# 23 blocks of rows in place of 24 in a mixture of experts, with a loop of four rounds and a tail of seven blocks

## The chip, the cores and the metric

The kernel runs on one core of a Trainium2 chip. A core has five engines with instruction streams of their own: TensorE (PE) multiplies matrices into eight banks of PSUM, VectorE (DVE), ScalarE (ACT) and GpSimd (POOL) work element by element, and SyncE (SP) issues DMA transfers. They meet only at semaphores. The metric is the time on the device in microseconds (us) of one execution; the lower the better.

## The reference, cut to what matters

Two layers run over 1024 rows of 256 numbers: attention over a context, then a mixture of experts, and the same once more with other weights. The change is in the first mixture of experts:

```python
logits = x @ router_w.T                                  # 8 experts
probs = softmax(logits)
top_w, top_i = top_k(probs, 2)
top_w = top_w / sum(top_w)
for e in range(8):
    gate, up = bitlinear(x, gate_w[e]), bitlinear(x, up_w[e])     # 256 -> 512
    y_e = bitlinear(up * square(relu(gate)), down_w[e])           # 512 -> 256
    out = out + combine[:, e:e + 1] * y_e
# bitlinear: weights rounded to -1, 0, 1 over their mean magnitude; each row of x
# rounded to integers of -128..127 over its largest magnitude
```

Each row goes to two of eight experts, so 2048 pairs of row and expert are worked on.

## The kernel before

The pairs are sorted by expert and cut into blocks of 128; the last block of each expert is filled up. `NBLK` blocks are always worked through, whatever the routing gives, and the blocks behind the last one in use compute on spare rows. 2048 pairs fill 16 blocks exactly, and each of eight experts can leave one block partly filled.

A block j goes through these steps, each on its engine:

- POOL gathers its 128 rows from DRAM into `xg[j % 4]` (line 570). Its program is one straight list: in step j it scales the hidden rows of block j - 7 (line 565), gathers block j and stores y of block j - 8 (line 577), as far as these blocks exist.
- TensorE turns the rows (`turn_rows`, line 763), ACT copies them out (`rows`, line 1220), TensorE multiplies by gate and up (`gate_up`, line 781). The expert comes from a register, since routing is known only while the kernel runs.
- ACT takes the relu of the gate (`relus`, line 1225), DVE squares, multiplies by up and finds the largest magnitude of each row for the rounding (`hidden`, lines 1579 to 1587), POOL scales.
- TensorE turns the hidden rows (`turn_hidden`, line 789), ACT rounds them (`hidden_rows`, line 1229), TensorE multiplies by down (`down`, line 796), ACT scales y out of PSUM (`outputs`, line 1235), and POOL stores it to the row's place in `y_rows`. ACT writes the y of a block only when the store of the block two before has landed.

Gate and up of a block lie in PSUM banks 1 and 3 if the block is even, in 2 and 4 if it is odd; bank 0 takes turned rows, bank 5 turned hidden rows, bank 6 y.

TensorE runs a prologue for blocks 0 to 3, then a hardware loop (`pe.Fori`) over rounds of four blocks, then a tail. In the part for block j stand `turn_hidden(j)`, `turn_rows(j + 4)`, `gate_up(j + 3)` and `down(j)`. A round loads one word from `run_e` into a register (`run_of`, line 771), which holds the experts of seven blocks, three bits each, and `in_run` shifts them out. With 24 blocks the loop has five rounds (blocks 0 to 19) and the tail four blocks (20 to 23). The tail loads a word again and also the last block's expert from `block_ei` (line 767). DVE has a loop too, over blocks 4 to 23 in five rounds; ACT and POOL have straight lists.

Behind block 20 and block 21 TensorE's list holds the first two pieces of the next job: folding the weights of the second layer's attention (`fold_queries` line 812, `fold_values` line 826, `fold_keys` line 841, for eight units u). `fold_values(0)` writes bank 1 and `fold_keys(0)` banks 3 and 1, so the last block must not use these. `fold_keys(0)` waits until y of the last block has been copied; the other folds follow. ACT and DVE copy each fold out. SP loads the weights of folds 1, 2, 3, 4 and 6 when the rows of blocks 5, 8, 11, 14 and 17 have been turned, and when all of y has landed it loads y back by rows (`yg`, line 511), from which DVE forms the layer's result and its normalisation.

Of the kernel before, what the change touches and what calls it, by code (L numbers as in the profile page):

```python
# [9 lines left out]
P = 128  # L10
# [11 lines left out]
FF = 512  # L22
NBLK = 24
RUN = 7
XROW = 258
QMAX = 127.0
# [71 lines left out]
def build(nc, x, ctx_in, cst_in, sel_in, kv_in, router_w, ffn_w, fold_in,  # L98
          weight_t, scale, masks_t, router_dt, out):
    with ExitStack() as ctx:  # L100
# [3 lines left out]
        def sb(name, shape, dt=F32):  # L104
            n = int(np.prod(shape[1:])) * (2 if dt == BF16 else 4)
            at = place[0]
            place[0] = (at + n + 31) // 32 * 32
            places[name] = at
            return nc.alloc_sbuf_tensor_at(name, shape, dt, offset=at)
# [50 lines left out]
        block_ei = sb("block_ei", [P, NBLK], U32)  # L160
        run_part = sb("run_part", [P, NBLK // 4 - 1])
        run_e = sb("run_e", [P, NBLK // 4 - 1], U32)
        below2 = sb("below2", [P, NBLK, NE])
# [208 lines left out]
        def rows_back(b):  # L372
            return (gathered[b], 16 * (NBLK // 4) + 16) if b < 4 else (sorted_back[b - 4], 16)

# [88 lines left out]
        def _(sp):  # L463
# [42 lines left out]
            for par in range(2):  # L506
                sp.wait_ge(y_stored[par], 16 * (NBLK // 2))
            y_by_tile = y_rows[0:2 * NT * P].rearrange("(k t p) d -> p k t d", k=2, p=P)
# [101 lines left out]
        def _(pe):  # L610
# [165 lines left out]
            def gate_up(j, par, e):  # L776
                pe.wait_ge(xgT_ready, j + 2)
                pe.wait_ge(hid_done, j + 1)
                for k in range(2):
                    for m in range(2):  # L780
                        mm = pe.matmul(bank[1 + 2 * m + par][:], xgT[par][:, k * P:(k + 1) * P],  # L781
                                       W[:, bass.ds(e, 1), m, k * FF:(k + 1) * FF].rearrange("p a i -> p (a i)"), start=k == 0, stop=k == 1)
                mm.then_inc(gu_ready, 1)
# [65 lines left out]
            pe.wait_ge(runs_ready, 1)  # L849
            with pe.Fori(0, NBLK // 4 - 1) as i:  # L850
                word = run_of(i)
                for r in range(4):
                    j = 4 * i + r
                    e_up, e_down = in_run(word, r + 3), in_run(word, r)
                    turn_hidden(j, r)
                    turn_rows(j + 4, i + 1, r)
                    gate_up(j + 3, (r + 1) % 2, e_up)
                    down(j, r % 2, e_down)
            word, last = run_of(NBLK // 4 - 2), expert_of(NBLK - 1)
            for j in range(NBLK - 4, NBLK):  # L860
                e_down = in_run(word, j - NBLK + 8) if j < NBLK - 1 else last
                turn_hidden(j, j % 4)
                if j + 3 < NBLK:
                    gate_up(j + 3, (j + 1) % 2, last)
                down(j, j % 2, e_down)
                if j == NBLK - 4:
                    fold_queries(0)
                if j == NBLK - 3:
                    pe.wait_ge(hid_done, NBLK + 1)
                    fold_values(0)  # L870
# [263 lines left out]
        def _(act):  # L1134
# [87 lines left out]
            def relus(j, par):  # L1222
                act.wait_ge(gu_ready, j + 1)
                act.wait_ge(hid_done, j + 1)
                act.activation(relu[par][:], bank[1 + par][:], ACT.Relu).then_inc(relu_ready, 1)

# [11 lines left out]
            for j in range(4):  # L1238
                rows(j, j % 2, j)
                if j:  # L1240
                    relus(j - 1, (j - 1) % 2)
            for i in range(NBLK // 4 - 1):
                for r in range(4):
                    j = 4 * i + r
                    hidden_rows(j, r % 2)
                    rows(j + 4, r % 2, r)
                    relus(j + 3, (r + 1) % 2)
                    outputs(j, 2 * i + r // 2, r % 2, r)
            for j in range(NBLK - 4, NBLK):
                hidden_rows(j, j % 2)  # L1250
                if j + 3 < NBLK:
                    relus(j + 3, (j + 1) % 2)
                outputs(j, j // 2, j % 2, j % 4)
# [40 lines left out]
            for u in range(NU):  # L1294
                if u == NU - 2:
                    for par in range(2):
                        act.wait_ge(y_stored[par], 16 * (NBLK // 2))
                fold(u)
# [73 lines left out]
        def _(dve):  # L1372
# [189 lines left out]
            dve.sem_inc(block_w_ready, 1)  # L1562
            seventh = 4 * (NBLK // 4 - 2) + 1
            so_far = block_e[:, RUN - 1:RUN - 1 + seventh:4]
# [8 lines left out]
            def hidden(j, r):  # L1573
# [4 lines left out]
                dve.wait_ge(relu_ready, j + 1)  # L1578
                link(dve.scalar_tensor_tensor(hid[r][:], bank[1 + par][:], 0.0, relu[par][:], ALU.max, ALU.mult))  # L1579
                dve.tensor_tensor(hid[r][:], hid[r][:], bank[3 + par][:], ALU.mult).then_inc(hid_done, 1)  # L1580
                dve.wait_ge(hid_done, j + 3)
# [7 lines left out]
            for j in range(4):  # L1589
                hidden(j, j)  # L1590
            with dve.Fori(1, NBLK // 4) as i:
                link.enter(i - 1, 16)
                for r in range(4):
                    hidden(4 * i + r, r)
                link.leave(NBLK // 4 - 1, 16)

# [339 lines left out]
```

## Time and profile before

| | |
|---|---|
| median of 3 runs | 512.0 us (511.37 to 514.07) |
| profiled execution, on the device | 510.0 us |
| its span in the trace | 508.2 us |
| PE busy | 384.1 us, 76% of the span |
| DVE busy | 362.7 us, 71% |
| ACT busy | 216.9 us, 43% |
| POOL busy | 146.6 us, 29% |
| the blocks of the first experts | from the first gather at 135.4 us to the last store at 223.8 us |

The shares are means over a span with many stages. What counts for one stage is read in it: which engine's step each other step waits for. In the timelines a row is one instruction (or several alike), with its start and its time in us and, in brackets, how long its engine had been idle and what ended that. "Issue" stands where the engine waited for nothing that the profile shows. TensorE's granted clock, PEclk, is a share of full speed.

### The profile page before, as it was taken

The numbers are of one execution on the slowest core, as the hardware profiler recorded it, in microseconds if no ns is written. First come the engines' busy times: TensorE is split into PE (matmuls) and PEld (weight loads), VectorE is DVE, ScalarE is ACT, GpSimd is POOL, SyncE is SP. The second block draws the span as 40 slices with busy tenths as digits, with TensorE's granted clock in tenths as the row PEclk, the third lists the DMA queues.
The fourth block names the chain that finished last, engine by engine and source line by source line (L and its number), as shares of the span: only waits on it lengthen the run. The fifth ranks groups of instructions, "written<-read, shape, count | busy, mean of one in ns | idle before, by whom it ended". The sixth has DMA issues, their size and how long they took to land.

```text
span 508.2 us, 10746 instructions
## 1 busy us (share of the span) xinstructions
PE 384.1 (76%) x3690; PEld 263.5 (52%) x3691; DVE 362.7 (71%) x892; ACT 216.9 (43%) x473; POOL 146.6 (29%) x156
## 2 busy tenths in 40 slices
PE   2567586734177766779798999999999989648892
PEld 1345465534134433547645656656656678536671
DVE  4999899995878977938677778768777535653451
ACT  2684988824055666647801122212212321225340
POOL 1082000000268887630003123213213320161422
PEclk9985978886588999979999999999999999859997
DMA  8964443041015545117102202201201201341000
GB/s 308 420 235 171 186 179 126 2 166 44 10 36 174 195 145 133 53 44 246 35 0 84 86 1 84 84 11 74 84 21 64 85 0 43 126 131 45 23 33 21
DMA packets 16974, 50.95 MB, mean 100 GB/s; under 512 B 2104, under 2 KB 6336, under 8 KB 14880
## 3 DMA queue, kind: packets, MB, share of 16 engines
q1 hardware_dynamic: 13984, 42.46, 23.3%
q0 software_dynamic: 2944, 7.88, 5.5%
q8 instruction: 29, 0.48, 0.4%
q14 instruction: 17, 0.14, 0.1%
HBM read 43.51 MB, written 6.82 MB: 99 GB/s over the span
## 4 chain that ended last, share of the span: by engine, by line
PE 52%; DVE 24%; issue 9%; POOL 7%; ACT 4%; DMA 3%; DVEq 0%; ACTq 0%; POOLq 0%
PE bank L913 14%; PE bank L1125 7%; PE bank L925 6%; PE bank L996 6%; DVE mx L1408 4%; PE bank L936 3%; DVE raw L1447 3%; PE bank L812 3%; POOL xg L570 2%; POOL y_rows L577 2%; POOL hid L565 2%; PE bank L972 2%; PE bank L949 2%; DVE W L1457 2%; PE bank L841 1%
## 5 line engine op out<-in xcount | busy, mean ns | idle before, releaser
L1623 DVE TENSOR_TENSOR roped<-bank,cst 128x512 f32<-128x512 f32 x96 | 61.7, 686 | 30.8 <-PE bank L913 29.3
L584 POOL TENSOR_TENSOR WE<-WE,wT 128x512 f32<-128x512 f32 x32 | 40.6, 1297 | 142.6 <-DMA WE<-_L_ffn_expert_masks_dram 142.6
L570 POOL DMA_INDIRECT xg<-x_rows,owner_b x24 | 24.2, 1007 | 99.5 <-DVE owner_b L413 93.5
L1281 ACT ACTIVATE qrT<-bank 128x512 f32<-128x512 f32 x16 | 8.7, 597 | 82.8 <-PE bank L936 82.8
L913 PE MATMUL bank<-XNT_hi,AW_hi 128*128 128x512 f32 x96 | 41.3, 430 | 2.3 <-DVE roped L1623 1.6
L913 PE MATMUL bank<-XNT_lo,AW_hi 128*128 128x512 f32 x96 | 37.8, 394 | 0.0
L913 PE MATMUL bank<-XNT_hi,AW_lo 128*128 128x512 f32 x96 | 37.8, 393 | 0.0
L925 PE MATMUL bank<-roped,MW 128*64 128x512 f32 x128 | 31.0, 605 | 0.0
L996 PE MATMUL bank<-VW,ctxT 128*128 128x256 f32 x128 | 30.8, 386 | 0.0
L913 PEld LDWEIGHTS bank<-XNT_hi,AW_hi 128*128 128x128 f32 x96 | 18.0, 187 | 22.0 <-DVE roped L1623 12.1
L577 POOL DMA_INDIRECT y_rows<-y,slot x24 | 23.8, 993 | 15.6 <-ACT y L1235 12.2
L781 PE MATMUL bank<-W,xgT 128*128 x96 | 27.0, 407 | 1.6 <-ACT xgT L1220 0.7
L789 PE MATMUL bank<-identf,hid 128*128 128x128 f32 x96 | 15.9, 289 | 15.0 <-POOL hid L565 13.6
L1164 ACT ACTIVATE W<-raw 128x1024 bf16<-128x1024 f32 x24 | 25.5, 1062 | 0.0
L1125 PE MATMUL bank<-WE,pT_d 128*128 x80 | 21.5, 411 | 4.7 <-DVE acc L1820 2.7
L996 PEld LDWEIGHTS bank<-VW,ctxT 128*128 128x128 f32 x128 | 23.2, 190 | 3.5 <-issue 0.8
L1229 ACT ACTIVATE hidT<-bank,less_magic 128x512 bf16<-128x512 f32 x24 | 16.5, 686 | 16.0 <-PE bank L789 14.8
L1579 DVE SCALAR_TENSOR_TENSOR hid<-bank,relu 128x512 f32<-128x512 f32 x24 | 16.5, 686 | 9.5 <-issue 5.0
L1150 ACT ACTIVATE pT<-bank 128x512 f32<-128x512 f32 x32 | 18.9, 598 | 9.4 <-PE bank L671 9.4
L671 PE MATMUL bank<-identf,pnat 128*128 128x128 f32 x128 | 21.6, 306 | 0.8 <-ACT pT L1150 0.8
L1408 DVE TENSOR_REDUCE mx<-bank 128x8 f32<-128x512 f32 x32 | 19.8, 680 | 3.1 <-PE bank L638 3.1
L796 PE MATMUL bank<-W,hidT 128*128 x96 | 16.3, 288 | 7.3 <-ACT hidT L1229 6.1
(294 smaller groups left out, 917.0 us busy)
## 6 DMA issues: line engine op xcount, KB each, us to landing
raw<-in_L_ffn_w_dram SPq DMA_DIRECT2D x8, 1536.0 KB, 7.1
fold<-in_L_xattn_fold_dram SPq DMA_DIRECT2D x8, 1024.0 KB, 8.0
WE<-_L_ffn_expert_masks_dram SPq DMA_DIRECT2D x8, 1024.0 KB, 5.4
kv<-in_keys_values_dram SPq DMA_DIRECT2D x8, 656.0 KB, 8.3
yg<-y_rows SPq DMA_DIRECT2D x8, 256.0 KB, 5.2
x_tok<-pay SPq DMA_DIRECT2D x8, 256.0 KB, 2.3
X<-in_x_dram SPq DMA_DIRECT2D x4, 256.0 KB, 9.1
ctx_sb<-in_ctx_dram SPq DMA_DIRECT2D x1, 768.0 KB, 18.5
```

What stands on the lines that cost most here:

```text
L570: pool.indirect_dma_start(out=xg[j % 4][:].bitcast(U32), out_offset=None, in_=x_rows, in_offset=bass.IndirectOffsetOnAxis(ap=RB.owner[:, j ...
L577: pool.indirect_dma_start(out=y_rows, out_offset=bass.IndirectOffsetOnAxis(ap=slot[:, b:b + 1], axis=0), in_=y[b % 2][:], in_offset=None). ...
L584: pool.tensor_tensor(WE[:, e], WE[:, e], wT[:], ALU.mult).then_inc(WE_ready, 1)
L671: mm = pe.transpose(bank[4 + kvl % 2][:, c * P:(c + 1) * P], pnat[kvl][:, c * P:(c + 1) * P], identf[:])
L781: mm = pe.matmul(bank[1 + 2 * m + par][:], xgT[par][:, k * P:(k + 1) * P], W[:, bass.ds(e, 1), m, k * FF:(k + 1) * FF].rearrange("p a i -> ...
L913: mm = pe.matmul(bank[g][:], a[:, k, c * P:(c + 1) * P], b[:, k, g * 512:(g + 1) * 512], start=k == 0 and i == 0, stop=k == 1 and i == 2)
L925: pe.matmul(bank[2 + g][half(h, g) * S:(half(h, g) + 1) * S, :], MW[u][:, r, at:at + S], roped[n][:, r, :], start=r == 0, stop=False, skip ...
L996: mm = pe.matmul(bank[t % 4][:, 0:H], ctxT[:, u, t * P:(t + 1) * P], VW[:, u, :], start=u == 0, stop=u == NU - 1)
L1125: mm = pe.matmul(bank[4 + r % 4][:, 0:H], pT_d[r % 4][:, k * P:(k + 1) * P], WE_k[:, bass.ds(e, 1), k, :].rearrange("p a o -> p (a o)"), s ...
L1164: ins = act.activation(W[:, e, m, :], raw[e % 3][:, m, :], ACT.Abs, accum_out=w_sum[e % 2][:, m:m + 1])
L1408: dve.tensor_reduce(mx[:, kvl, :], bank[kvl][:].rearrange("p (h s) -> p h s", s=S), AX.X, ALU.max).then_inc(nat_read, 1)
L1623: ins = dve.tensor_tensor(roped[n][:, r, :].rearrange("p (b s) -> p b s", s=S), src, cst[:, None, at:at + S].to_broadcast([P, 8, S]), ALU. ...
```

## The change

`NBLK` becomes 23. TensorE's loop has `ROUNDS` = 4 rounds (blocks 0 to 15) and its tail seven blocks (16 to 22), whose experts all come from one word of `run_e`; the load of the last block's expert is gone. DVE's loop covers blocks 4 to 19 in four rounds, and blocks 20 to 22 are straight code. Since the last block is now even, the banks of even and odd blocks are exchanged: even ones use 2 and 4, odd ones 1 and 3. Waits that counted half of an even number of blocks now count what there is of each kind. The fold pieces stand behind blocks 19 and 20.

```diff
-NBLK = 24
+NBLK = 23
 RUN = 7
+ROUNDS = (NBLK - RUN) // 4
...
-                sp.wait_ge(y_stored[par], 16 * (NBLK // 2))
+                sp.wait_ge(y_stored[par], 16 * len(range(par, NBLK, 2)))
...
-                        mm = pe.matmul(bank[1 + 2 * m + par][:], xgT[par][:, k * P:(k + 1) * P],
+                        mm = pe.matmul(bank[2 + 2 * m - par][:], xgT[par][:, k * P:(k + 1) * P],
...
-            with pe.Fori(0, NBLK // 4 - 1) as i:
+            with pe.Fori(0, ROUNDS) as i:
...
-            word, last = run_of(NBLK // 4 - 2), expert_of(NBLK - 1)
-            for j in range(NBLK - 4, NBLK):
-                e_down = in_run(word, j - NBLK + 8) if j < NBLK - 1 else last
+            word = run_of(ROUNDS)
+            for k in range(RUN):
+                j = 4 * ROUNDS + k
                 turn_hidden(j, j % 4)
+                if j + 4 < NBLK:
+                    turn_rows(j + 4, ROUNDS + 1 + k // 4, j % 4)
                 if j + 3 < NBLK:
-                    gate_up(j + 3, (j + 1) % 2, last)
-                down(j, j % 2, e_down)
+                    gate_up(j + 3, (j + 3) % 2, in_run(word, k + 3))
+                down(j, j % 2, in_run(word, k))
                 if j == NBLK - 4:
                     fold_queries(0)
                 if j == NBLK - 3:
...
-            with dve.Fori(1, NBLK // 4) as i:
+            with dve.Fori(1, ROUNDS + 1) as i:
                 link.enter(i - 1, 16)
                 for r in range(4):
                     hidden(4 * i + r, r)
-                link.leave(NBLK // 4 - 1, 16)
+                link.leave(ROUNDS, 16)
+            for j in range(4 * ROUNDS + 4, NBLK):
+                hidden(j, j % 4)
```

TensorE at the end of its loop, before (the last down product of the round, the branch, then the tail's first turn):

```order
L796 MATMUL bank<-W,hidT_154 128x256
L850 REGISTER_ALU
L850 COMPARE_AND_BRANCH
L771 TENSOR_LOAD run_e
L771 ISA x2
L767 TENSOR_LOAD block_ei
L767 ISA x2
L789 MATMUL bank<-identf,hid_149 128x128 x4
L781 ISA
```

The same place after, now behind block 15 and not behind block 19:

```order
L797 MATMUL bank<-W,hidT_154 128x256
L851 REGISTER_ALU
L851 COMPARE_AND_BRANCH
L772 TENSOR_LOAD run_e
L772 ISA x2
L790 MATMUL bank<-identf,hid_149 128x128 x4
L764 MATMUL bank<-ident,xg_141 128x128 x2
L782 REGISTER_ALU x2
```

One of the two register loads is gone, and the turn of the block's rows four ahead stands in the tail too.

TensorE from `fold_values(0)` to the down product of the next block, before (block 22; `hid_151` is the third of four buffers):

```order
L826 MATMUL bank<-fold_201 64x256 x2
L789 MATMUL bank<-identf,hid_151 128x128 x4
L796 REGISTER_ALU x2
L796 ISA
L796 MATMUL bank<-W,hidT_153 128x256
```

and after (block 21, second buffer):

```order
L827 MATMUL bank<-fold_201 64x256 x2
L790 MATMUL bank<-identf,hid_150 128x128 x4
L797 ISA
L797 MATMUL bank<-W,hidT_154 128x256
L797 ISA
```

The two register instructions that found the expert are no longer there, since the register that gate and up used is used again.

POOL around its last gather, before (the gather into `xg_144` is that of block 23):

```order
L565 TENSOR_SCALAR hid_152<-hid_152,hs_110 128x512
L570 DMA xg_143<-x_rows,owner_b 128x129
L577 DMA y_rows<-y_155,slot 5120x256
L565 TENSOR_SCALAR hid_149<-hid_149,hs_107 128x512
L570 DMA xg_144<-x_rows,owner_b 128x129
L577 DMA y_rows<-y_156,slot 5120x256
L565 TENSOR_SCALAR hid_150<-hid_150,hs_108 128x512
```

and after:

```order
L566 TENSOR_SCALAR hid_152<-hid_152,hs_110 128x512
L571 DMA xg_143<-x_rows,owner_b 128x129
L578 DMA y_rows<-y_155,slot 4992x256
L566 TENSOR_SCALAR hid_149<-hid_149,hs_107 128x512
L578 DMA y_rows<-y_156,slot 4992x256
L566 TENSOR_SCALAR hid_150<-hid_150,hs_108 128x512
```

The gather between the scaling of block 16 and the store of block 15 is gone.

## Rows read from the trace of the kernel before

**Rows 1.** The chain of waits from 128 to 252 us, shares by engine and line.

```profile
by line: issue 19.0%; PE bank L812 10.6%; POOL xg L570 9.8%; POOL y_rows L577 9.3%; POOL hid L565 8.8%; PE bank L841 6.0%; DMA y_rows<-y,slot 5.2%; PE bank L826 4.1%; PE bank L796 3.3%; PE bank L789 2.4%; DMA xg<-x_rows,owner_b 2.2%; PE ban
```

**Rows 2.** Timeline of POOL, blocks 15 to 17 and the last store (start us, us, ...).

```profile
199.75 0.71 POOL L565 TENSOR_SCALAR hid<-hid,hs 128x512 f32<-128x512 f32 x1
200.63 1.01 POOL L570 DMA_INDIRECT xg<-x_rows,owner_b  x1 [0.17 <-issue]
201.95 0.99 POOL L577 DMA_INDIRECT y_rows<-y,slot  x1 [0.30 <-issue]
202.98 0.70 POOL L565 TENSOR_SCALAR hid<-hid,hs 128x512 f32<-128x512 f32 x1
...
223.83 0.97 POOL L577 DMA_INDIRECT y_rows<-y,slot  x1 [1.10 <-ACT y L1235]
```

**Rows 3.** Timeline of PE around two starts of a round.

```profile
160.62 0.66 PE L789 MATMUL bank<-identf,hid 128*128 128x128 f32 x4 [1.31 <-POOL hid L565]
...
199.16 0.65 PE L796 MATMUL bank<-W,hidT 128*128 x4 [1.03 <-ACT hidT L1229]
200.97 0.65 PE L789 MATMUL bank<-identf,hid 128*128 128x128 f32 x4 [1.16 <-POOL hid L565]
...
202.60 0.65 PE L796 MATMUL bank<-W,hidT 128*128 x4
203.74 0.65 PE L789 MATMUL bank<-identf,hid 128*128 128x128 f32 x4 [0.49 <-POOL hid L565]
```

**Rows 4.** Timeline of PE, the last blocks: turns (L789), down products (L796), folds.

```profile
208.71 0.66 PE L789 MATMUL bank<-identf,hid 128*128 128x128 f32 x4 [0.42 <-POOL hid L565]
...
212.19 0.65 PE L789 MATMUL bank<-identf,hid 128*128 128x128 f32 x4 [1.29 <-issue]
...
213.91 0.65 PE L796 MATMUL bank<-W,hidT 128*128 x4 [0.21 <-issue]
...
218.54 0.66 PE L789 MATMUL bank<-identf,hid 128*128 128x128 f32 x4
220.27 0.66 PE L796 MATMUL bank<-W,hidT 128*128 x4 [1.07 <-ACT hidT L1229]
220.77 0.60 PE L789 MATMUL bank<-identf,hid 128*128 128x128 f32 x4
222.24 0.81 PE L796 MATMUL bank<-W,hidT 128*128 x4 [0.86 <-ACT hidT L1229]
223.60 1.55 PE L841 MATMUL bank<-fold 64*128 64x64 f32 x12 [0.56 <-ACT y L1235]
```

**Rows 5.** Timeline of DVE: first step of block 20, last of block 22.

```profile
206.65 0.69 DVE L1579 SCALAR_TENSOR_TENSOR hid<-bank,relu 128x512 f32<-128x512 f32 x1 [0.38 <-PE bank L789]
...
214.91 0.20 DVE L1587 TENSOR_SCALAR hs<-hs 128x1 f32<-128x1 f32 x1
```

**Rows 6.** Windows (busy us of each engine, then PEclk, DMA share, GB/s).

```profile
222.00:223.00 1.00, 0.77 (x4) 0.39 (x4) 0.00 (x0) 0.10 (x1) 0.72 (x1) 0.79 0.00 0
226.00:229.00 3.00, 3.00 (x13) 1.81 (x11) 1.03 (x3) 0.98 (x2) 0.00 (x0) 0.50 0.10 32
229.00:230.00 1.00, 1.00 (x15) 0.93 (x13) 0.12 (x1) 0.00 (x0) 0.00 (x0) 0.80 1.07 365
```

**Rows 7.** Timelines of PE, DVE and ACT behind the blocks.

```profile
225.08 2.93 PE L812 MATMUL bank<-fold 128*128 128x192 f32 x8
...
229.98 1.57 PE L812 MATMUL bank<-fold 128*128 128x192 f32 x8
...
232.88 1.57 PE L812 MATMUL bank<-fold 128*128 128x192 f32 x8
...
246.34 0.17 DVE L1652 SCALAR_TENSOR_TENSOR less_mean_q<-mv,rstd 128x8 f32<-128x8 f32 x1
...
248.28 2.07 ACT L1301 ACTIVATE XN<-X,less_mean_q,rstd 128x256 f32<-128x256 f32 x4
```

**Rows 8.** Timeline of DVE in the sorting ahead of the blocks.

```profile
130.64 0.31 DVE L409 TENSOR_SCALAR of_block_b<-of_block_b,cst 128x384 bf16<-128x384 bf16 x1
```

More of the change, by code:

```diff
@@ L160, in build @@
         block_ei = sb("block_ei", [P, NBLK], U32)
-        run_part = sb("run_part", [P, NBLK // 4 - 1])
-        run_e = sb("run_e", [P, NBLK // 4 - 1], U32)
+        run_part = sb("run_part", [P, ROUNDS + 1])
+        run_e = sb("run_e", [P, ROUNDS + 1], U32)
         below2 = sb("below2", [P, NBLK, NE])
@@ L372, in rows_back @@
         def rows_back(b):
-            return (gathered[b], 16 * (NBLK // 4) + 16) if b < 4 else (sorted_back[b - 4], 16)
+            return (gathered[b], 16 * len(range(b, NBLK, 4)) + 16) if b < 4 else (sorted_back[b - 4], 16)
         def row(a, t):
@@ L1224, in relus @@
                 act.wait_ge(hid_done, j + 1)
-                act.activation(relu[par][:], bank[1 + par][:], ACT.Relu).then_inc(relu_ready, 1)
+                act.activation(relu[par][:], bank[2 - par][:], ACT.Relu).then_inc(relu_ready, 1)
             def hidden_rows(j, par):
@@ L1241, in _ @@
                     relus(j - 1, (j - 1) % 2)
[L1242 to L1249, printed above, removed]
+            for j in range(NBLK):
                 hidden_rows(j, j % 2)
+                if j + 4 < NBLK:
+                    rows(j + 4, j % 2, j % 4)
                 if j + 3 < NBLK:
-                    relus(j + 3, (j + 1) % 2)
+                    relus(j + 3, (j + 3) % 2)
                 outputs(j, j // 2, j % 2, j % 4)
@@ L1296, in _ @@
                     for par in range(2):
-                        act.wait_ge(y_stored[par], 16 * (NBLK // 2))
+                        act.wait_ge(y_stored[par], 16 * len(range(par, NBLK, 2)))
                 fold(u)
@@ L1562, in _ @@
             dve.sem_inc(block_w_ready, 1)
-            seventh = 4 * (NBLK // 4 - 2) + 1
+            seventh = 4 * ROUNDS + 1
             so_far = block_e[:, RUN - 1:RUN - 1 + seventh:4]
@@ L1578, in hidden @@
                 dve.wait_ge(relu_ready, j + 1)
-                link(dve.scalar_tensor_tensor(hid[r][:], bank[1 + par][:], 0.0, relu[par][:], ALU.max, ALU.mult))
-                dve.tensor_tensor(hid[r][:], hid[r][:], bank[3 + par][:], ALU.mult).then_inc(hid_done, 1)
+                link(dve.scalar_tensor_tensor(hid[r][:], bank[2 - par][:], 0.0, relu[par][:], ALU.max, ALU.mult))
+                dve.tensor_tensor(hid[r][:], hid[r][:], bank[4 - par][:], ALU.mult).then_inc(hid_done, 1)
                 dve.wait_ge(hid_done, j + 3)
```

## The prediction

> **What bounds the kernel now.** I read the page first for where the expert blocks lie, then the chain of waits over that stretch, then the engines' timelines block by block, and last the granted clock. The chain from 128 to 252 us [rows 1] is the thing to see first: it is no single engine. POOL's three steps per block (gather, scaling, store of y) hold some 28% of it, TensorE's fold groups (L812, L841, L826) 21%, and 19% is "issue", time in which nothing shown was waited for. So the stretch has two regimes, which the timelines separate.
>
> In the **steady regime** POOL sets the pace: from the scaling of block 16 at 199.75 to that of block 17 at 202.98 lie 3.23 us, filled by scaling, gather and store with fixed gaps between them [rows 2]. POOL gathers seven blocks ahead of its scaling, so after the gather of block 23 at 200.63 nothing is left to gather. Then the **drain** begins: eight stores of y, the last at 223.83 [rows 2], and the ring POOL (scale) - TensorE (turn, down) - ACT (copy y) - POOL (store, then the scaling after the next) sets the pace, with two blocks under way. Near its end TensorE alone is late: its turn of block 20 stands at 212.19 behind 1.29 us of "issue" [rows 4], which is the exit from the round loop with its two register loads. From there to fold_keys(0) at 223.60 [rows 4], the first piece of TensorE's next job, are 11.41 us: four blocks, the first with a gate/up, and two pieces of fold between them. After 223.60 TensorE runs fold on fold, and that stretch moves as a whole with its start: the loads of folds 1 to 6 hang on block counts of the middle of the loop, and the loads of yg on the last stores of y.
>
> **The change part by part.** The sum is made on the profiled execution: 510.0 us on the device, 508.2 us of it span, 1.8 around it. The median of the runs shown is 512.0, 2.0 above that execution; I subtract the saving from the median.
>
> *The prologue.* Tables of 24 columns become 23. The DVE group at 130.64 [rows 8] shrinks by a twenty-fourth, 0.01 us; if its width 16 x 23 lost whatever lets it be quick, it could double, +0.31. The row is contiguous and its total stays even, so I take 0.
>
> *Up to the store of block 14* nothing changes: the same gathers, stores and fold loads stand in the same order, and the exchanged banks alternate exactly as before (even blocks now write 2 and 4, odd ones 1 and 3), so each bank has the same writer and reader one block apart. I cost the exchange at nothing; its purpose is that the last block, now even, leaves banks 1 and 3 to the first fold.
>
> *The gather of block 23 goes.* On POOL this frees 1.02 us and its gap ahead of the store of block 15, so that store and the scaling of block 17 come about 1.2 us sooner. Not all of it reaches TensorE. Its turn of block 16 at 200.97 does not wait for the gather but for the loop's edge: the down product of block 15 ends at 199.16 + 0.65 = 199.81, and 1.16 us pass [rows 3]. The down product of block 16 ends at 202.60 + 0.65 = 203.25, and only then can block 17 be turned, which happened at 203.74 after 0.49 us of waiting for POOL [rows 3]. So the odd ring gains at most 0.49 and at least nothing; I take 0.4, since nothing else in the ring is late. The turn of block 19 moves from 208.71 [rows 4] to 208.3.
>
> *The loop's exit moves from block 20 to block 16.* At block 16 a back edge stood already, 1.16 us [rows 3]; an edge at the start of round 1 shows 1.31 idle [rows 3], part of it POOL's. The exit at block 20 with two register loads took 1.29 [rows 4]. So the new exit, with one load, costs what the old edge did within 0.15 us, and the 1.29 us in the drain has no successor: the tail is straight code. Here a rule bears: the Trainium skill (Runtime: NRT & Kernel Launch, Instruction fetch mechanics) says that code is prefetched in sequence and that a taken branch to a place not held costs a fetch. By it an exit, which falls through, should be cheaper than a back edge, block 16 could be turned up to 0.46 us sooner, and the time would be 507.3. The trace does not bear it out: the fall-through took 1.29 and the taken edge 1.16. The sum goes without it.
>
> *The last four blocks.* The new drain makes the same sequence from the turn of block 19 (gate/up of the last block, fold_queries(0), fold_values(0), three blocks without a gate/up) as the old one from block 20. It took 11.41. Three of the old blocks computed their expert's address between hidT and the down product: block 22 needed 220.27 - 218.54 = 1.73 from turn to down, block 23, whose expert was in a register, 222.24 - 220.77 = 1.47 [rows 4]. In the tail of the changed program no register instruction stands there for blocks 20 to 22. That is worth 0 to 3 x 0.26 = 0.78; I take 0.5, as some of it is hidden where POOL is late. So fold_keys(0) starts at 208.3 + 10.9 = 219.2, against 223.60: 4.4 us sooner. The bounds are 208.71 + 11.41 = 220.12 (3.5) and 208.22 + 10.63 = 218.85 (4.75).
>
> *What is late next: DVE.* In the drain it works back to back. Its last step of block 22 is at 214.91 + 0.20 = 215.11 [rows 5], and it doesn't move, as blocks 20 to 22 follow each other there without idle time. POOL's scaling (0.70) and some gaps put the turn of block 22 at 215.9 at the earliest, and from the last turn to fold_keys(0) lie 223.60 - 220.77 = 2.83 [rows 4]: 218.7. So 0.5 us of slack is left where there was plenty. DVE leaves its loop after block 19 now, in the middle of this. At its back edge into block 20 stand 0.38 us of idle [rows 5], which the profile puts to a turn of TensorE's that was long done; what an exit costs is not shown where it could be seen, and TensorE's cost 1.29. The exit replaces an edge, so it costs up to 0.9 more, and the end is 218.7 to 219.6; if it costs less than the edge, up to 0.38, that only widens the slack. I allow 0.2 for it and **take 4.2 us**, with 3.5 to 4.75 for the ends.
>
> *Behind it.* The fold stretch, the yg loads and all later stages hang on one another; none waits for a fixed time. 510.0 - 4.2 = 505.8 for an execution like the profiled one, and **507.8 from the median**.
>
> **The rivals.**
>
> *A. TensorE's clock stays up.* The granted clock falls to half (1.2 of 2.4 GHz) between 222 and 223 us, after a stretch in which TensorE waited for ACT and POOL between the last blocks, and is back, fold upon fold, between 229 and 230 [rows 6]. That costs real time: the unit of folds from 225.08 took 4.90 us, the next one, from 229.98, 2.90 [rows 7], and fold_keys(0) its share, 2.7 in all. A tighter drain could keep the clock up. The gain is capped, since ACT's normalisation at 248.28 then waits for DVE's less_mean_q at 246.34 + 0.17 instead [rows 7]: 1.8 us. Time 506.0. Against it: the waits between the last three blocks are the same as before.
>
> *B. The drain gives less.* If DVE's or TensorE's exit costs more than an edge and the last blocks wait for it, only one block of the drain is saved: 220.77 - 218.54 = 2.23 [rows 4]. Time 509.8. For it speaks the half microsecond of slack on DVE; against it that the 1.29 us have to come back in a place where POOL's pace covers them.
>
> *C. Slower: the longer straight tail starves TensorE's sequencer.* The tail's instructions are new code for three more blocks; if each of seven blocks paid a gap as at the old exit, 7 x 1.29 = 9.0 us come back, 4.8 more than is saved: 516.8. It turns slower by more than 0.5% from (4.2 + 2.6) / 1.29 = 5.3, so six blocks on. Against it: in the old tail block 21 to 23, straight code too, show no such gap [rows 4].
>
> *D. It does nothing:* the stretch behind the blocks is set by something that does not move, such as the load of the last folds. Time 512.0. Against it: TensorE's fold groups follow each other without a wait for DMA [rows 7].
>
> **How the numbers follow.** The forecast has 0.62, A 0.14, B 0.16, C 0.04, D 0.04. A measurement of this kernel can tell about 0.5%, 2.6 us, from no change. Faster by more than that, below 509.4: forecast and A with a little of B, 0.78. Same: most of B, D and a few hundredths of the forecast, 0.18. Slower: C, 0.04. The range: down to A with the upper bound of the saving and the lowest run shown (0.6 under the median), 512.0 - 4.75 - 1.8 - 0.6 = 504.8; up to B with the same 0.6 and a little, 510.5.
>
> **What would show it.** Right: 23 gathers; about 1.2 us ahead of TensorE's turn of block 16 and no gap of over 1 us of "issue" ahead of a later turn; from the turn of block 19 to fold_keys(0) under 11.4 us, and the folds behind it closed up. DVE's last step of block 22 within a microsecond of POOL's last scaling. Wrong: a gap after DVE's block 19 of more than a microsecond (B), gaps in TensorE between L796 and L789 in each tail block (C), full clock through 220 to 226 us (A), or a fold group that waits for a DMA (D).

## The result and the profile after

| | before | after |
|---|---|---|
| median of the runs, same chip | 512.97 us (511.37 to 514.07) | 505.12 us (503.45 to 505.93) |
| ratio, 95% interval | | 0.9854 [0.9811, 0.9896] |
| profiled execution, on the device | 510.0 us | 505.9 us |
| its span in the trace | 508.2 us | 504.1 us |

The change makes the kernel faster by 1.5%, 7.9 us in these runs. In two later groups of runs the same changed kernel came to 505.18 and 504.73 us beside 511.65 and 512.43 (0.9869 [0.9834, 0.9905] and 0.9861 [0.9815, 0.9906]), so 6.5 to 7.9 us. The median of before is here that of four runs, 1.0 us above the 512.0 of three that the forecast started from. One execution of before_warm2, a run further down, took 1221 us; it is in that run's median and left out of its ratio. The forecast was 507.8, with 504.8 to 510.5 for the range: sign right, saving too small by some 3 us.

The two profiled executions lie only 4.1 us apart, and that invites a wrong reading: the forecast said 4.2. Two stages have to be kept apart, so I read the trace in pieces. As a zero point I take the down product of block 15, the last one ahead of the place where the loop's exit now stands. The timeline of TensorE after the change, from there to the folds (start us, us, engine, line, op, out<-in; in brackets the idle time ahead and what ended it):

```profile
199.74 0.65 PE L797 MATMUL bank<-W,hidT 128*128 x4 [1.08 <-ACT hidT L1232]
201.09 0.66 PE L790 MATMUL bank<-identf,hid 128*128 128x128 f32 x4 [0.70 <-POOL hid L566]
...
202.72 0.65 PE L797 MATMUL bank<-W,hidT 128*128 x4
203.21 0.60 PE L790 MATMUL bank<-identf,hid 128*128 128x128 f32 x4
...
207.69 0.65 PE L797 MATMUL bank<-W,hidT 128*128 x4
208.18 0.63 PE L790 MATMUL bank<-identf,hid 128*128 128x128 f32 x4
...
209.67 0.65 PE L797 MATMUL bank<-W,hidT 128*128 x4
...
211.47 0.60 PE L790 MATMUL bank<-identf,hid 128*128 128x128 f32 x4
...
213.51 0.65 PE L827 MATMUL bank<-fold 128*64 128x256 f32 x4
214.10 0.65 PE L790 MATMUL bank<-identf,hid 128*128 128x128 f32 x4
...
217.69 0.65 PE L797 MATMUL bank<-W,hidT 128*128 x4 [0.86 <-ACT hidT L1232]
218.91 1.29 PE L842 MATMUL bank<-fold 64*128 64x64 f32 x12 [0.56 <-ACT y L1238]
```

These rows answer to [rows 3] and [rows 4]. From the down product of block 15 to fold_keys(0) lie 218.91 - 199.74 = 19.17 us; before they were 223.60 - 199.16 = 24.44. So the blocks gave 5.27 us. The 1.29 us of "issue" that stood in the drain have no successor there: the turn of block 19 (208.18) follows the down product of block 18 (207.69) with no idle time in brackets, and so do the turns of blocks 20 and 21, each behind a piece of fold.

POOL over the place of the lost gather, answering to [rows 2]:

```profile
199.30 0.99 POOL L578 DMA_INDIRECT y_rows<-y,slot  x1 [1.13 <-ACT y L1238]
200.33 0.71 POOL L566 TENSOR_SCALAR hid<-hid,hs 128x512 f32<-128x512 f32 x1
201.21 1.01 POOL L578 DMA_INDIRECT y_rows<-y,slot  x1 [0.18 <-issue]
202.26 0.71 POOL L566 TENSOR_SCALAR hid<-hid,hs 128x512 f32<-128x512 f32 x1
...
215.41 0.70 POOL L566 TENSOR_SCALAR hid<-hid,hs 128x512 f32<-128x512 f32 x1
...
219.13 0.98 POOL L578 DMA_INDIRECT y_rows<-y,slot  x1 [1.00 <-ACT y L1238]
```

From one scaling to the next are 1.93 us where 3.23 stood. The last store is at 219.13, 4.7 us sooner than before.

The second piece is the folds, with TensorE's clock. Windows (us, busy us of PE, PEld, DVE, ACT, POOL with counts, then the granted clock, DMA share, GB/s), answering to [rows 6]:

```profile
219.00:220.00 1.00, 1.00 (x12) 1.00 (x12) 0.73 (x2) 0.61 (x2) 0.87 (x1) 0.61 0.04 12
220.00:222.00 2.00, 2.00 (x8) 1.88 (x8) 1.08 (x3) 0.57 (x2) 0.10 (x1) 0.50 0.18 66
222.00:223.00 1.00, 1.00 (x6) 0.71 (x6) 0.56 (x1) 0.36 (x2) 0.00 (x0) 0.69 0.26 44
```

The granted clock still falls to its lower level, 1.2 GHz, at the start of the folds, but it is back between 222 and 223, some 3 us on; before it stayed down for 6 to 7 us. The stretch from fold_keys(0) to ACT's normalisation answers to [rows 7]:

```profile
240.91 0.17 DVE L1652 SCALAR_TENSOR_TENSOR less_mean_q<-mv,rstd 128x8 f32<-128x8 f32 x1
```
```profile
242.53 2.07 ACT L1299 ACTIVATE XN<-X,less_mean_q,rstd 128x256 f32<-128x256 f32 x4
```

That is 242.53 - 218.91 = 23.62 us, and it was 24.68. Both pieces together: 42.79 where 49.12 stood, 6.3 us. The profiled execution shows only 4.1 of them, because a later stage of it was slower: from the normalisation to the end of the span it took 504.1 - 242.53 = 261.57 us where the one of before took 508.2 - 248.28 = 259.92. Two more traces of each kind, below, show that this part varies by itself.

### The profile page after: what moved, and what is told of

It is laid out like the page before. It is cut to its first block, busy times and chain, and to the rows that moved or that the text cites. A ratio compares the mean times of both kernels' runs of the same rounds, so it can differ in the third digit from the quotient of the medians.

```text
span 504.1 us, 10636 instructions
## 1 busy us (share of the span) xinstructions
PE 380.5 (75%) x3670; PEld 262.5 (52%) x3677; DVE 359.8 (71%) x885; ACT 214.7 (43%) x468; POOL 144.0 (29%) x153
## 4 chain that ended last, share of the span: by engine, by line
PE 52%; DVE 24%; issue 8%; POOL 8%; ACT 4%; DMA 3%; DVEq 0%; ACTq 0%; POOLq 0%
PE bank L916 14%; PE bank L1128 8%; PE bank L928 6%; PE bank L999 6%; DVE mx L1406 4%; PE bank L939 3%; DVE raw L1445 3%; PE bank L813 3%; POOL y_rows L578 2%; POOL xg L571 2%; POOL hid L566 2%; PE bank L975 2%; PE bank L952 2%; DVE W L1455 2%; DVE W L1449 1%
## 5 line engine op out<-in xcount | busy, mean ns | idle before, releaser
L782 PE MATMUL bank<-W,xgT 128*128 x86 | 24.5, 408 | 2.2 <-issue 1.1
L1820 DVE SCALAR_TENSOR_TENSOR dg<-bank,row_w,dg 128x256 f32 x20 | 9.7, 484 | 17.4 <-PE bank L1128 9.3
L1128 PE MATMUL bank<-WE,xT 128*128 x76 | 19.8, 399 | 2.8 <-ACT xT L1365 2.0
```

The costliest lines, as they stand in the source:

```text
L782: mm = pe.matmul(bank[2 + 2 * m - par][:], xgT[par][:, k * P:(k + 1) * P], W[:, bass.ds(e, 1), m, k * FF:(k + 1) * FF].rearrange("p a i -> ...
L1128: mm = pe.matmul(bank[4 + r % 4][:, 0:H], pT_d[r % 4][:, k * P:(k + 1) * P], WE_k[:, bass.ds(e, 1), k, :].rearrange("p a o -> p (a o)"), s ...
```

## The experiments

Two questions were open. The first: where do the blocks' 5.3 us come from, when 4.2 were forecast? The second: is the shorter spell of half clock a gain in time, and why does it differ? Ratios are against the kernel before on the same chip.

**The two kernels again.** No edit.

> The changed kernel once more, with more rounds. Theory S (the saving is made in the drain of the blocks and is the same in each execution): fold_keys(0) starts 4.5 to 5 us sooner than in the kernel before, as in the first two traces (218.91 against 223.60), and the ratio is 0.985 to 0.991. Theory L (the 7.5 us between the medians are partly luck in where TensorE's clock drops, since the two profiled executions lie only 4.1 us apart): with more rounds the ratio moves up to about 0.991, 4.5 us.

> The kernel before against itself, for the scatter and a second trace. Both theories: ratio 1.000 within its interval. Theory S: fold_keys(0) at 223 to 224 us again. Theory L: the second trace shows spells of half clock in other places than the first, in the last stage (430 to 465 us) above all, and a span some us longer than 508.2, near the median less 1.8, about 510 to 511.

> The changed kernel a third time, beside the two others. If the whole saving is made from block 14's turn to the normalisation, as the first four traces say (55.0 and 55.1 us against 48.7 and 48.5), that stage takes 48 to 50 us and the ratio is 0.986 to 0.988; if the stages behind give part of it back, the ratio is above 0.989.

Measured: after 505.18 and 504.73 us, ratios above; the kernel before against itself 512.41, 1.0016 [0.9988, 1.0043], so 0.4% is what such a comparison can tell. The ratios of the changed kernel are those of theory S, but the saving in the drain is not the same in each execution (19.17 and 20.60 us below). The span of before_again, 510.8 us, is what theory L expected, but not for its reason: the last stage (430 to 465 us) has the same granted clock, 0.76, in both traces of before. Block 14's turn to the normalisation took 46.8 us in after_third, less than the 48 to 50 expected. The pieces in all five traces, each column the time from one row to another:

| trace | down product of block 15 to fold_keys(0) | fold_keys(0) to normalisation | sum | normalisation to the end of the span |
|---|---|---|---|---|
| before | 24.44 | 24.68 | 49.12 | 259.92 |
| before_again | 24.33 | 24.84 | 49.17 | 261.03 |
| after | 19.17 | 23.62 | 42.79 | 261.57 |
| after_again | 20.60 | 22.00 | 42.60 | 260.74 |
| after_third | 19.13 | 22.00 | 41.13 | 258.57 |

The whole saving lies in the first two columns: 49.15 against 42.17 on the mean, 7.0 us, which is what the medians say (6.5 to 7.9). The last column goes from 258.57 to 261.57 within the changed kernel alone and shows no difference of the two kinds; that is what shrank the first pair's distance to 4.1. In after_again the spell of half clock sat in the drain (0.52 in the window 201 to 204), and the turn of block 17 came 204.43 - 199.56 = 4.87 us behind the zero point, not 3.47: the spell costs 1.4 there. In after_third there is none in either place:

```profile
219.13 0.89 PE L842 MATMUL bank<-fold 64*128 64x64 f32 x12 [0.56 <-ACT y L1238]
219.95 1.57 PE L813 MATMUL bank<-fold 128*128 128x192 f32 x8
...
222.84 1.57 PE L813 MATMUL bank<-fold 128*128 128x192 f32 x8
```
```profile
220.00:222.00 2.00, 2.00 (x14) 1.41 (x12) 1.73 (x5) 1.32 (x3) 0.33 (x1) 1.00 0.18 66
```

One unit of folds after another takes 2.90 us from the first on, where [rows 7] show 4.90 for it.

**tail8: the loop alone.** The kernel before, with 24 blocks and all its gathers, but four rounds and a straight tail of eight:

```diff
-            with pe.Fori(0, NBLK // 4 - 1) as i:
+            with pe.Fori(0, ROUNDS) as i:          # ROUNDS = 4
...
-            word, last = run_of(NBLK // 4 - 2), expert_of(NBLK - 1)
-            for j in range(NBLK - 4, NBLK):
+            word, last = run_of(ROUNDS), expert_of(NBLK - 1)
+            for k in range(NBLK - 4 * ROUNDS):
+                j = 4 * ROUNDS + k
...
+                if j + 4 < NBLK:
+                    turn_rows(j + 4, ROUNDS + 1 + k // 4, j % 4)
...
-            with dve.Fori(1, NBLK // 4) as i:
+            with dve.Fori(1, ROUNDS + 1) as i:
...
+            for j in range(4 * ROUNDS + 4, NBLK):
+                hidden(j, j % 4)
```

> 24 blocks, but with the loop of four rounds and a straight tail of eight blocks: the part of the change that moves the exit, alone. My theory: the 1.29 us at the exit in the drain and some of the address instructions go, so fold_keys(0) comes 1.5 to 2.2 us sooner than in the kernel before and the time is 1.5 to 2.2 us less, ratio about 0.996. Rival (the saving is the block's own pace on POOL, 3.2 us, and the exit is hidden anyway): no difference, ratio 1.000. Rival (the block is worth only the last 2.2 us and the exit most of the rest): 4 us or more, ratio 0.992.

Measured: 509.46 us, 0.9962 [0.9943, 0.9980], so 1.9 us faster with 1.0 to 2.9 for the interval; the rivals' ratios, 1.000 and 0.992, lie outside it. Its TensorE, and the scaling of block 16 on POOL:

```profile
200.23 0.65 PE L797 MATMUL bank<-W,hidT 128*128 x4 [1.21 <-ACT hidT L1232]
202.20 1.11 PE L790 MATMUL bank<-identf,hid 128*128 128x128 f32 x4 [1.31 <-POOL hid L566]
...
213.29 0.66 PE L790 MATMUL bank<-identf,hid 128*128 128x128 f32 x4 [0.63 <-POOL hid L566]
...
224.24 0.89 PE L842 MATMUL bank<-fold 64*128 64x64 f32 x12 [0.56 <-ACT y L1238]
```
```profile
200.82 0.71 POOL L566 TENSOR_SCALAR hid<-hid,hs 128x512 f32<-128x512 f32 x1
```

Here the exit at block 16 keeps two register loads and takes 1.31 us. POOL's scaling had ended at 201.53, so 0.67 of that is TensorE's own. In the changed kernel the exit has one load, the idle time is 0.70, and the turn starts at 201.09, 0.05 us behind POOL's scaling (200.33 + 0.71): there the exit is hidden, and costs 0.7 at most. At the same place the second load thus adds 0.6 or more. The last four blocks, 224.24 - 213.29 = 10.95, are 0.46 shorter than the 11.41 of before. The trace as such reaches fold_keys(0) 24.01 us behind the zero point, only 0.4 sooner than before; a spell of half clock sat in its drain (the turn of block 16 takes 1.11 us, not 0.65). With the 1.4 that such a spell cost in after_again it would be 1.8 sooner, an estimate that fits the median.

**loads: what a register load costs.** The changed kernel, with the exit's loads put back into the straight tail, where there is no loop; their values are not used:

```diff
             for k in range(RUN):
                 j = 4 * ROUNDS + k
+                if k == 3:
+                    run_of(ROUNDS)
+                if k == 5:
+                    run_of(ROUNDS)
+                    expert_of(NBLK - 1)
                 turn_hidden(j, j % 4)
```

> The changed kernel with register loads put back into TensorE's tail, without a branch: one ahead of the turn of block 19, two ahead of the turn of block 21; the loaded values are not used. If the gap of 1.29 us at the old exit was its two loads: about 0.6 of idle ahead of the turn of block 19 and 1.2 to 1.3 ahead of that of block 21, and 1.5 to 1.9 us more in all. If it was the loop's edge (branch and code behind it): 0.1 or less at both, and the same time.

Measured: 506.59 us beside 505.18 for the changed kernel in the same group, 0.9910 [0.9881, 0.9939]; 1.4 us more, a little under the 1.5 to 1.9 of the first theory.

```profile
200.33 0.65 PE L797 MATMUL bank<-W,hidT 128*128 x4 [0.97 <-ACT hidT L1237]
...
208.26 0.65 PE L797 MATMUL bank<-W,hidT 128*128 x4
209.32 0.65 PE L790 MATMUL bank<-identf,hid 128*128 128x128 f32 x4 [0.40 <-issue]
...
214.69 0.65 PE L827 MATMUL bank<-fold 128*64 128x256 f32 x4
...
215.95 0.65 PE L790 MATMUL bank<-identf,hid 128*128 128x128 f32 x4 [0.61 <-issue]
...
220.74 0.89 PE L842 MATMUL bank<-fold 64*128 64x64 f32 x12 [0.56 <-ACT y L1243]
```

With one load the turn of block 19 starts 1.06 us behind the down product, and 0.49 without (208.18 - 207.69 in after): 0.57 for one load. With two, the turn of block 21 starts 1.26 us behind the fold, and 0.59 without (214.10 - 213.51): 0.67 for both. That is not a price of 0.1 for the second: these two stand behind a fold of 0.65 us and not behind a down product, and how much of them the fold hid is not shown. Where two loads and one stand at the same place, the second adds 0.6 or more (tail8 and after, above). The Trainium skill (DMA: Bandwidth & Descriptors, Latency and other measured facts) gives a floor of some 600 ns for a `tensor_load`; for one load the trace agrees with 0.57. From the zero point to fold_keys(0) are 220.74 - 200.33 = 20.41 us, against 19.15 (mean of the two undisturbed traces): 1.26 later, which is the sum of the two pieces, 1.24, to the last hundredths. From block 19 on TensorE has no slack in this drain. The old exit was mostly its two loads: from the down product to the turn it took 212.19 - 210.23 = 1.96 us (210.23 from the same timeline as [rows 4]), 1.47 more than the 0.49 of straight code. The exit with one load took 1.35 at most, 0.86 more; less the 0.57 for that load, 0.29 at most is left for the exit itself. This last step is a subtraction between runs and not a run of its own.

**gather: POOL's last gather put back.** The changed kernel, with a 24th gather of rows that nothing reads:

```diff
                 if j < NBLK:
                     pool.indirect_dma_start(out=xg[j % 4][:].bitcast(U32), ...)
+                if j == NBLK:
+                    pool.wait_ge(xgT_ready, j - 2)
+                    pool.wait_ge(gathered[j % 4], 16 * (j // 4))
+                    pool.indirect_dma_start(out=xg[j % 4][:].bitcast(U32), ...)
```

> The changed kernel with POOL's last gather put back: between the scaling of block 16 and the store of block 15 POOL gathers block 22's rows once more, into the buffer that block 19 has left; nothing uses them. My theory as the two traces of the changed kernel correct it: the store of block 15 and the scaling of block 17 come 1.2 us later, the turn of block 17 waits for POOL again, and of the 1.05 us that the odd ring gained (turn 14 to turn 19: 15.43 us before, 14.38 after) some 0.5 to 1.05 are lost; turn 14 to fold_keys(0) 25.6 to 26.2, and 0.5 to 1 us in the time. Rival (the gather is a block's price at POOL's pace): 1.2 us or more. Rival (the gather is hidden and the loop's exit alone made the gain): none.

Measured: 506.50 us, 0.9905 [0.9868, 0.9943].

```profile
201.47 1.02 POOL L576 DMA_INDIRECT xg<-x_rows,owner_b  x1 [0.17 <-issue]
...
203.83 0.71 POOL L566 TENSOR_SCALAR hid<-hid,hs 128x512 f32<-128x512 f32 x1
```
```profile
200.00 0.65 PE L802 MATMUL bank<-W,hidT 128*128 x4 [0.69 <-ACT hidT L1237]
...
202.98 0.65 PE L802 MATMUL bank<-W,hidT 128*128 x4
204.59 0.66 PE L795 MATMUL bank<-identf,hid 128*128 128x128 f32 x4 [0.96 <-POOL hid L566]
...
220.46 1.55 PE L847 MATMUL bank<-fold 64*128 64x64 f32 x12 [0.56 <-ACT y L1243]
```

The gather moves the scaling of block 17 back behind itself, and TensorE's turn of block 17 waits 0.96 us for it. That turn comes 204.59 - 200.00 = 4.59 us behind the zero point (down product of block 15 at 200.00 here), 1.1 later than in after. At fold_keys(0) it is 1.3 us (20.46 against 19.15), 0.13 of it because the clock began to fall under the last down product (0.78 us in place of 0.65). The medians of different groups put it at 1.3 to 1.8 us, and the interval of the ratio overlaps that of the changed kernel; the size rests on the trace. That is more than the 0.5 to 1 expected, and by its number the first rival's ("1.2 us or more"). The path is the expected one (26.0 us from the turn of block 14 to fold_keys(0), 25.6 to 26.2 expected): one added wait, ahead of the turn of block 17; the only later wait of a turn for POOL, 0.41 us, has its like in after (0.39).

**warm and warm2, before_warm and before_warm2: the clock held up.** Into the changed kernel and into the one before, the same products that nothing reads, in the waits of the last two blocks and ahead of fold_keys(0):

```diff
+            def keep_busy(n):
+                for _ in range(n):
+                    pe.matmul(bank[3][:].rearrange("p (a n) -> p a n", a=4), ident[:], ident[:, None, :].to_broadcast([P, 4, P]), start=True, stop=True)
...
                 turn_hidden(j, j % 4)
+                if j > NBLK - 3:
+                    keep_busy(4)
...
+            keep_busy(2)
             pe.wait_ge(y_copied, NBLK + 1)
             fold_keys(0)
```

> The changed kernel with matrix products added that nothing reads, while TensorE waits in its last two blocks: four behind each of the last two turns, two ahead of fold_keys(0), all into bank 3, which is free there. Theory C (the clock's spell of half speed at the first folds is set by TensorE's waiting between the last blocks, and costs up to 2.7 us): full clock from 210 to 245 us, fold_keys(0) to ACT's normalisation 22.0 us as in the second trace of the changed kernel, against 23.6 in the first; 0 to 1.5 us less time, since that kernel is without the spell in some executions. Rival (the products delay the down products behind them as much as the clock gives back): the same time or up to 1 us more.

> The kernel before with the same added products in its last two blocks. Theory C: both its traces show the spell in the same place and 6.6 us long, so full clock there gives back all of it: fold_keys(0) to ACT's normalisation 22.0 us against 24.7, 2 to 2.7 us less time, ratio 0.995; and the blocks' own part of the change is then the distance between this kernel and the changed one with the same products, about 4 to 4.5 us. Rival (the change's whole gain lies in the blocks, the clock only shifts): no difference, and the distance stays at 6.6 us.

> The changed kernel with the added products again, beside the changed kernel on the same chip. C1: 0.5 to 1.5 us below it. C2: the same time within 0.7 us. In both the stage from block 14's turn to the normalisation takes 48 to 49 us.

> The kernel before with the added products again, since its first trace gained 2.3 us from block 14's turn to ACT's normalisation (52.72 against 55.0) while its median did not gain. Theory C1 (the gain at the folds is real, and what the first look's times showed was scatter): stage 52.7 again, ratio 0.995 to 0.998. Theory C2 (the clock only moves its spell: what the folds gain is lost where TensorE waits later, at the normalisation and ahead of the last stage, 4.75 for 3.93 us and 35.0 for 33.3 us in the first trace): stage 52.7 again, those two stretches long again, ratio 1.000 to 1.003.

Measured: before_warm 512.01 us, 1.0020 [0.9993, 1.0047], and 510.72, 0.9975 [0.9945, 1.0005]; warm 504.38 us, 0.9861 [0.9830, 0.9891], and 504.42, 0.9855 [0.9819, 0.9890]. In the trace the edit does what it is meant to. TensorE and ACT of before_warm:

```profile
224.83 0.89 PE L841 MATMUL bank<-fold 64*128 64x64 f32 x12
225.65 1.57 PE L812 MATMUL bank<-fold 128*128 128x192 f32 x8
```
```profile
247.16 2.07 ACT L1308 ACTIVATE XN<-X,less_mean_q,rstd 128x256 f32<-128x256 f32 x4 [0.19 <-DVE less_mean_q L1659]
```

The first fold unit takes 1.57 us for its eight products, not 2.93 as in [rows 7], and the normalisation comes 22.33 us behind fold_keys(0), as in before_warm2, instead of 24.68 and 24.84: 2.4 us sooner, and then it waits 0.19 for DVE's less_mean_q. But the medians don't show it: the two ratios lie on either side of 1, and their mean is 0.9998. The reason can be read in wider windows. One line of before, two of before_warm, two of before_warm2:

```profile
222.00:230.00 8.00, 7.20 (x41) 5.41 (x41) 2.97 (x6) 2.69 (x7) 1.70 (x2) 0.57 0.27 91
```
```profile
248.00:252.00 4.00, 3.44 (x17) 3.25 (x17) 1.80 (x4) 3.04 (x7) 0.00 (x0) 0.57 0.00 0
415.00:419.00 4.00, 4.00 (x14) 3.18 (x14) 1.50 (x5) 0.10 (x1) 1.70 (x2) 0.57 0.00 0
```
```profile
202.00:207.00 5.00, 4.70 (x23) 3.12 (x24) 3.59 (x9) 2.70 (x6) 3.23 (x4) 0.66 0.20 41
250.00:255.00 5.00, 4.99 (x22) 4.03 (x21) 2.84 (x5) 2.51 (x5) 0.00 (x0) 0.66 0.00 0
```

A stretch of 8 us at a granted clock of 0.57 holds 8 x 2 x 0.43 = 6.9 us at half clock. In all three traces the rest of 195 to 425 us shows 1.00. So with the products TensorE was at half clock for as long as without them (6.9 and 6.8 us), only elsewhere: the products moved the half clock and didn't lessen it, which is theory C2. In before_warm both pieces lie behind the normalisation, and from there to the end of the span it took 262.34 us (259.92 and 261.03 without products). In before_warm2 one lies in the drain (25.27 us from zero point to fold_keys(0), 0.9 more than without it), the other behind the normalisation (260.64). On the changed kernel the edit is worth nothing that can be measured, and there was little to win: its folds lost 1.6, 0 and 0 us to the clock in three traces. With the products in both kernels their medians lie 7.6 and 6.3 us apart, and not the 4 to 4.5 of theory C: that is the number of its rival.

What the clock gives the changed kernel in the median is therefore **not settled**. The traces put it at 2.2 us of the 7.0 (24.76 against 22.54 on the mean), less 0.5 for the spell in the drain of after_again. But a spell that leaves the folds can come back elsewhere: counted as above, the changed kernel was at half clock between 195 and 425 us for 3.4 us in after, 6.9 in after_again and 0 in after_third, and after had a further 3.4 us at 454 to 459. That is less than the kernel before had, in three traces only. Why the spell falls into the drain in some executions and on the folds in others was not tried.

None of these versions is clearly faster than the changed kernel.

## Why the prediction was right, and where its sizes were off

Everything is counted from the down product of block 15.

- **Which regimes bound the stretch: right.** A drain that is a ring with TensorE late in it, behind a regime paced by POOL. loads shows it directly: 1.24 us put on TensorE in the drain come out as 1.26 at fold_keys(0). One count was off: behind the last gather before stand nine stores of y (blocks 15 to 23), not eight.
- **The exit leaves the drain, one block's period of 3.48 us goes: right.** It was the largest term, 212.19 - 208.71 in [rows 4].
- **"The new exit, with one load, costs what the old edge did": wrong, and this is the step that failed.** The turn of block 16 came 201.09 - 199.74 = 1.35 us behind the zero point, before 200.97 - 199.16 = 1.81: 0.46 sooner, and held there by POOL. I had compared an exit with two loads (1.29) with an edge with one (1.16) and read them as equal. tail8 shows an exit with two loads at the same place at 1.31, the changed kernel one with one load at 0.70 or less, against 1.16 for the taken edge with one load. The rule that I set aside there, the Trainium skill's (Runtime: NRT & Kernel Launch, Instruction fetch mechanics), says that a taken branch to a place not held costs a fetch. By it the fall-through should be the cheaper one; with the loads made equal the trace agrees, and my sentence that it doesn't was wrong. That the difference is instruction fetch no run here shows: the head of a round also computes its addresses and semaphore counts from the round's number, which the tail has as constants, and no run parts the two.
- **The gather gone, "the odd ring gains at most 0.49": the bound was wrong for the same reason.** The turn of block 17 came 1.11 us sooner: 0.46 of it handed on from block 16, and 0.65 from its own wait for POOL (0.49 of idle before; now it starts 0.16 ahead of the modelled end of the down product). The 1.2 us by which POOL comes sooner could be used nearly in full, and gather, which takes them back, costs 1.1 there. The exit's part needs the gather's: with the gather in place the turn of block 16 still comes 1.35 us behind the zero point, but that of block 17 at 4.59, as in before (4.58). Turn of block 19: 208.18 - 199.74 = 8.44 against 9.55, 1.11 sooner, predicted 0.4.
- **The last four blocks: right.** 218.91 - 208.18 = 10.73 and 10.71 in after_third, 10.9 predicted with 10.63 for the bound. Of the 0.69 us some 0.14 are the clock's: before, it began to fall under the last down product, which took 0.81 us [rows 4]; in before_again, where it didn't, the last four blocks took 11.29 and not 11.41. Some 0.55 is left for the register instructions, where 0.5 was taken.
- **DVE as the next late engine: harmless.** It left its loop without a gap:

```profile
206.19 0.21 DVE L1585 TENSOR_SCALAR hs<-hs 128x1 f32<-128x1 f32 x1
206.44 0.69 DVE L1577 SCALAR_TENSOR_TENSOR hid<-bank,relu 128x512 f32<-128x512 f32 x1
...
214.53 0.21 DVE L1585 TENSOR_SCALAR hs<-hs 128x1 f32<-128x1 f32 x1
```

  The last step of block 19 ends at 206.40 and block 20 starts at 206.44, where 0.38 us stood at the back edge [rows 5]. The 0.2 allowed for it were not needed. Its last step of block 22 lies 0.7 us ahead of POOL's last scaling, as was said.
- **Sum of the blocks:** 3.48 + 1.11 + 0.69 = 5.28 us, measured 5.27 and, in after_third, 5.31; forecast 4.2 with 4.75 for the upper end. The blocks alone went past their upper end; that the time still fell into the range is owed to the 1.8 us for rival A and the 0.6 for scatter that stood in its lower bound.
- **Rival A, the clock: in the traces it came in part, and its cap was wrong.** It was put at 0.14 and at 1.8 us. The clock stayed up through the folds in two of three traces, and then fold_keys(0) to normalisation took 22.00 us, 2.7 to 2.8 less, the whole price of the spell. I had held less_mean_q fixed in time; it comes sooner too. In after_third:

```profile
240.37 0.17 DVE L1652 SCALAR_TENSOR_TENSOR less_mean_q<-mv,rstd 128x8 f32<-128x8 f32 x1
```
```profile
240.61 0.66 ACT L1269 ACTIVATE MW<-bank 128x256 f32<-128x256 f32 x2
241.13 2.08 ACT L1299 ACTIVATE XN<-X,less_mean_q,rstd 128x256 f32<-128x256 f32 x4
```

  It lies 21.24 us behind fold_keys(0), before 246.34 - 223.60 = 22.74; what lets it come sooner was not traced, and ACT's own last copies are the later ones there. A cap of this kind shows only in before_warm and before_warm2 (waits of 0.19 and 0.20 for less_mean_q), at 2.35 and not at 1.8.
- **Rival B** fell: no gap behind DVE's block 19, and the saving is over one period. **C** fell: behind the exit no turn of the tail waits with "issue" ahead of it; the one wait is 0.39 us for POOL, at block 18. **D** fell: no fold waits for a DMA, and all later stages moved along.

So of the 3 us by which the saving was too small, 1.1 are in the blocks: 0.7 from the exit's price and the wait for POOL behind it, 0.2 in the last four blocks, most of it the clock's, and 0.2 allowed for DVE. The rest goes by the traces to the clock at the folds; what that is worth in the median stays open.

## What to carry to other kernels

Where a loop's exit stands matters more than what it costs: move it out of the drain, where one engine has no slack, to a place where another engine's pace covers it, and take its register loads out of it. When two control transfers are compared, make the instructions that they carry equal first. And a saving is read between two rows that both kernels have: two profiled executions 4.1 us apart hid one of 7, because another stage varied by 3 us between executions of the same kernel.

## What the hardware showed that was not expected

- One register load on TensorE delays it by 0.57 us in straight code (loads). A second one at the loop's exit adds 0.6 or more (1.31 us of idle time in tail8, at most 0.70 in after).
- TensorE's taken back edge with one load shows 1.16 us [rows 3], its exit with one load at most 0.70, its exit with two 1.29 to 1.31.
- The spell at half clock near the end of the blocks has no fixed place: on the folds in both traces of before (2.7 us lost), on the folds for half as long in after, in the drain in after_again (1.4 us lost), warm and before_warm2, in both in tail8, in neither in after_third.
- Products that nothing reads, put into TensorE's waits, kept the granted clock up over the folds in all four traces, and made no difference in the medians that could be measured: in both traces of the kernel before the half clock came back elsewhere, for 6.8 to 6.9 us as without them.
